# A GRU's difference step that builds its state before its difference, and squares that are issued behind the other set's gates

## The reference, cut to what matters

```
def cell(h, x):
    gi = x @ W_ih + b_ih
    gh = h @ W_hh + b_hh
    r = sigmoid(i_r + h_r)
    z = sigmoid(i_z + h_z)
    n = tanh(i_n + r * h_n)
    h_new = (1.0 - z) * n + z * h
```

## Time and profile before

| what | value |
|---|---|
| median of 3 runs | 2480.27 us (2479.81 to 2484.01) |
| the profiled execution's own time | 2479.73 us |
| its span, first to last instruction | 2478.2 us |
| mean granted TensorE clock | 0.977 |
| busy over the span: PE, DVE, ACT, POOL | 94%, 53%, 27%, 8% |
| L867, `old_less` | 42 instructions, 17.9 us |
| L876, `diff` | 42 instructions, 17.9 us |
| L881, transpose to `hi` | 42 instructions, 18.7 us |
| L731, squares with their accumulator reads | 42 each, 17.4 and 7.5 us |

### The profile page before, as it was taken

How to read it: one execution, slowest core, us unless ns; L and a number is a source line. 1 busy time by engine, 2 the same in 40 slices (tenths; PEclk the granted TensorE clock), 3 DMA queues, 4 the chain that set the end, 5 groups by cost and what they waited for, 6 DMA issues and landing times. The chain is left out here.

```text
span 2478.2 us, 83692 instructions
## 1 busy us (share of the span) xinstructions
PE 2335.3 (94%) x35300; PEld 1277.8 (52%) x35300; DVE 1303.3 (53%) x2691; ACT 661.4 (27%) x1333; POOL 210.6 (8%) x440
## 2 busy tenths in 40 slices
PE   7999999999999989999999999999999999967736
PEld 3444444444444445455666656666666666633312
DVE  4322121212122357777666655666666666888877
ACT  3200000000001123333333333333333333355530
POOL 0000000000000000000000000111111111122225
PEclk9999999999999999999999999999999999999965
DMA  7693131313132445444444443444444444477730
GB/s 236 208 332 127 52 127 52 127 52 127 51 144 103 153 150 152 141 138 134 137 135 135 135 134 101 120 119 116 114 119 119 115 116 118 122 215 232 229 93 5
DMA packets 177335, 330.61 MB, mean 133 GB/s; under 512 B 24272, under 2 KB 87168, under 8 KB 176192
## 3 DMA queue, kind: packets, MB, share of 16 engines
q1 hardware_dynamic: 145360, 267.53, 34.4%
q10 hardware_dynamic: 24192, 44.05, 4.8%
q0 software_dynamic: 7680, 17.57, 4.4%
HBM read 222.39 MB, written 156.77 MB: 153 GB/s over the span
## 5 line engine op out<-in xcount | busy, mean ns | idle before, releaser
L581 PE MATMUL banks<-w_hi,hi 128*32 128x512 f16 (+1 forms) x13824 | 605.0, 328 | 55.7 <-DVE hi L881 43.0
L581 PEld LDWEIGHTS banks<-w_hi,hi 128*32 128x32 f16 x13824 | 359.8, 97 | 284.8 <-DVE hi L881 53.7
L314 DVE SCALAR_TENSOR_TENSOR out_stage<-acc,bias_row 128x512 f32<-128x512 f32 x168 | 116.1, 691 | 622.0 <-PE acc L372 622.0
L581 PE MATMUL banks<-w_hi,lo 128*32 128x512 f16 (+1 forms) x8192 | 354.9, 326 | 0.0
L581 PE MATMUL banks<-w_lo,hi 128*32 128x512 f16 (+1 forms) x8192 | 354.9, 326 | 0.0
L370 PE MATMUL acc<-w_hi,x_even 128*128 128x512 f16 x768 | 291.7, 380 | 13.5 <-DVE x_even L306 11.1
L371 PE MATMUL acc<-w_hi,x_even 128*128 128x512 f16 x768 | 291.6, 380 | 0.0
L372 PE MATMUL acc<-w_lo,x_even 128*128 128x512 f16 x768 | 291.6, 380 | 0.0
L581 PEld LDWEIGHTS banks<-w_lo,hi 128*32 128x32 f16 x8192 | 217.8, 97 | 115.0
L581 PEld LDWEIGHTS banks<-w_hi,lo 128*32 128x32 f16 x8192 | 217.8, 97 | 115.0
L707 ACT ACTIVATE rz<-sums 128x512 f32<-128x512 f32 x176 | 110.9, 630 | 534.5 <-DVE sums L846 534.3
(11 more groups left out here) (172 smaller groups left out, 2162.8 us busy)
## 6 DMA issues: line engine op xcount, KB each, us to landing
stage<-gi_scratch SPq DMA_DIRECT2D x704, 96.0 KB
gi_scratch<-out_stage ACTq DMA_DIRECT2D x168, 256.0 KB, 2.0
stage<-sums_scratch SPq DMA_DIRECT2D x40, 512.0 KB
stage<-in_xT SPq DMA_DIRECT2D x32, 512.0 KB, 6.6
y<-in_x_rows SPq DMA_DIRECT2D x32, 512.0 KB, 4.3
hs_scratch<-h SPq DMA_DIRECT2D x128, 128.0 KB
x_keep<-hs_scratch SPq DMA_DIRECT2D x32, 512.0 KB, 3.9
y<-hs_scratch POOLq DMA_DIRECT2D x32, 512.0 KB
```

The costliest lines, as they stand in the source:

```text
L314: nc.vector.scalar_tensor_tensor(out=out_stage[:, tb], in0=acc[e % BANKS][:], scalar=UNSCALE, in1=bias_row[:].rearrange("p q f -> p (q f)" ...
L581: last = nc.tensor.matmul(bank[q * COLS:(q + 1) * COLS, 0:b - a], state[:, s, j], w[:, j, q * QW + a:q * QW + b], start=first and j == 0, ...
```

## The change

In a DIFFS or LAST step DVE no longer makes `old_less`. It makes the state first (`h` = `new_n` + `z_old`) and then the difference from the state, 256 h less the saved state, and transposes it. On ACT the square of a set's difference is no longer issued behind that set's own tanh, but behind the gates of the other set's next step, in front of the tanh there; the last one of the pass stands behind the loop. The square writes its unused elementwise output into `lo` and not into `rz`.

```diff
-            if mode in (DIFFS, LAST):
-                dve.wait_ge(z_old_ready[s], n)
-                dve.wait_ge(warm_state_loaded[s][u], from_diffs(it) * 8 + 16 * (1 + u))
-                nc.vector.scalar_tensor_tensor(out=old_less[:, s], in0=z_old[:, s], scalar=S_SCALE, in1=warm_state[:, s, u],
-                                               op0=ALU.mult, op1=ALU.subtract).then_inc(old_less_ready[s], 1)
             dve.wait_ge(not_z_ready[s], n)
             dve.wait_ge(n_ready[s], n)
             nc.vector.tensor_tensor(new_n[:, s], not_z[:, s], n_act[:, s], ALU.mult).then_inc(new_n_ready[s], 1)
             dve.wait_ge(z_old_ready[s], n)
             dve.wait_ge(new_n_ready[s], n)
-            if mode in (DIFFS, LAST):
-                dve.wait_ge(old_less_ready[s], from_diffs(it) + (u + 2))
-                nc.vector.scalar_tensor_tensor(out=diff[s], in0=new_n[:, s], scalar=S_SCALE, in1=old_less[:, s],
-                                               op0=ALU.mult, op1=ALU.add).then_inc(diff_made[s], 1)
-                dve.wait_ge(diff_made[s], from_diffs(it) + (u + 2))
-                if mode == DIFFS:
-                    dve.wait_ge(diff_seen[s], from_diffs(it) + (u + 1))
-                nc.vector.transpose(flat(hi[:, s]), diff[s]).then_inc(hi_ready[s], 1)
             if mode not in (HEADS, KEPT):
                 dve.wait_ge(h_stored[s][u], it * 16 + (16 - pair_of(0, 0) * 16))
             if mode == KEPT:
                 dve.wait_ge(state_out_ready[s], it * 2 + (u + 1 - WARM_HEADS))
             nc.vector.tensor_tensor(h_new, new_n[:, s], z_old[:, s], ALU.add).then_inc(h_ready[s], 1)
+            dve.wait_ge(h_ready[s], n)
             if mode in (DIFFS, LAST):
+                dve.wait_ge(warm_state_loaded[s][u], from_diffs(it) * 8 + 16 * (1 + u))
+                nc.vector.scalar_tensor_tensor(out=diff[s], in0=h_new, scalar=S_SCALE, in1=warm_state[:, s, u],
+                                               op0=ALU.mult, op1=ALU.subtract).then_inc(diff_made[s], 1)
+                dve.wait_ge(diff_made[s], from_diffs(it) + (u + 2))
+                if mode == DIFFS:
+                    dve.wait_ge(diff_seen[s], from_diffs(it) + (u + 1))
+                nc.vector.transpose(flat(hi[:, s]), diff[s]).then_inc(hi_ready[s], 1)
                 return
```

```diff
         def act_diff(act, it, u, s):
             act.wait_ge(hi_ready[s], steps_to(it, u) + 2)
-            nc.scalar.activation(rz[:, s, 0:QF], flat(hi[:, s]), ACT.Square,
+
+            nc.scalar.activation(flat(lo[:, s]), flat(hi[:, s]), ACT.Square,
...
-                    act_step(act, it, 1, 0, turns, modes[1], after_tanh=lambda: act_squares(act, T))
-                    if first and modes[1] != FULL:
-                        act_diff(act, it, 1, 0)
...
+                    def gates(u, s, then=None):
+
+                        def after():
+                            if modes[u * s] in (DIFFS, LAST):
+                                act_diff(act, it - 1 if (u, s) == (0, 0) else it, u if s else 1 - u, 1 - s)
+                            if then:
+                                then()
+                        return after
...
+                    act_step(act, it, 1, 0, turns, modes[1], gates(1, 0), lambda: act_squares(act, T))
...
                     with act.Fori(DIFF_TILE, TILES) as i:
                         tile(i, (DIFFS, DIFFS), True)
+                    act_diff(act, pair_of(p, TILES - 1), 1, 1)
```

More of the change, by code:

```diff
@@ L473, in recurrence @@
     new_n = n_sum
-    old_less = sums[:, :, 0:QF]
     diff = [sums[:, s, RZ:RZ + QF // 2].bitcast(F16) for s in range(SETS)]
@@ L517, in recurrence @@
         set_sems(n) for n in ("sums_stored", "gi_kept", "state_out_ready", "state_stored", "diff_seen"))
-    old_less_ready, diff_made = set_sems("old_less_ready"), set_sems("diff_made")
+    diff_made = set_sems("diff_made")
     curves_loaded, split_step = sem("curves_loaded"), sem("split_step")
@@ L794, in tile @@
                     it, T = pair_of(p, i), p * TILES + i
[L795 to L800, removed]
-                    act_step(act, it, 1, 0, turns, modes[1], after_tanh=lambda: act_squares(act, T))
-                    if first and modes[1] != FULL:
-                        act_diff(act, it, 1, 0)
[L804 to L807, removed]
+                    def gates(u, s, then=None):
[5 more added lines that the diff above has]
+                        return after
+                    act_step(act, it, 0, 0, turns, modes[0], gates(0, 0), (lambda: act_signs(act, T - 1)) if routed else None)
+                    act_step(act, it, 0, 1, turns, modes[0], gates(0, 1), lambda: act_sum(act, T))
+                    act_step(act, it, 1, 0, turns, modes[1], gates(1, 0), lambda: act_squares(act, T))
+                    act_step(act, it, 1, 1, turns, modes[1], gates(1, 1, (lambda: act_hit(act, T - 1, i - 2)) if routed else None),
+                             lambda: act_normalise(act, T, i - 1))
                 tile(1, (FULL, FULL), False)
@@ L886, in dve_step @@
             nc.vector.tensor_tensor(h_new, new_n[:, s], z_old[:, s], ALU.add).then_inc(h_ready[s], 1)
+            dve.wait_ge(h_ready[s], n)
             if mode in (DIFFS, LAST):
+                dve.wait_ge(warm_state_loaded[s][u], from_diffs(it) * 8 + 16 * (1 + u))
[5 more added lines that the diff above has]
+                nc.vector.transpose(flat(hi[:, s]), diff[s]).then_inc(hi_ready[s], 1)
                 return
-            dve.wait_ge(h_ready[s], n)
             nc.vector.transpose(flat(h_turned[:, s]), h_new).then_inc(turned[s], 1)
```

## The result

The changed kernel takes 2476.82 us, the kernel before 2480.30 us beside it (20 runs each): ratio 0.9983, 95% interval 0.9977 to 0.9989. It is faster, by 3.5 us and not by the 14.2 forecast, and outside the range of 2460.5 to 2472.

The account below looks back on a forecast made before the run. DVE, nearly full and waiting for the gates, was taken as the bound, not PE. Ten tiles x 0.96 plus nine x 0.51 gave 14.2 us, from 2479.73 to 2465.5, as a median 2466.0; range 2460.5 to 2472.

Parts of the forecast that it names:

- Both waits for the gates: DVE's rn in steps (1,b) and (0,b) would stop waiting for ACT's gates: 0.91 and 0.92 us a tile.
- 0.12 us a tile: In DVE's steps, removing old_less and lengthening the dependent chain would cancel, leaving 0.12 us a tile.
- rival 1, transfers set the tile: In the DIFFS tiles, transfers no denser than 0.85 would hold the tile at 19.8 us: gain 7.4, 2473; chance 0.13.
- nothing queues behind it: On SP, the next load's wait for `hi_ready` follows h by 0.9 us, and nothing would queue behind it.
- The forecast tile of 19.07: A DIFFS tile would shorten from 20.54 to 19.07 us, by 1.47.
- L905 comes at R+5.86+1.27: With R rn's start in (1,a), L905 waits for POOL's normalisation and comes at R+7.13, not R+7.64: gain 0.51.
- nine times 0.51: Gain in the tile's other half, up to L905, in nine of ten tiles: 4.6 us.
- only one tile in ten is late, and as late as before: In the one late tile POOL already sets L905, which waited 0.69 us for the normalisation; that half gains nothing there.
- Rival 4: Later `hi` closes the loop through PE's product and the gates to rn: 13 us lost, 2493; chance 0.07.

Follow-up runs that it names:

- e8: Kernel before with ACT's half of the change only, POOL's scale and shift ahead of its gathers, and late tiles' copies of x issued early: 2465.69 us, 0.9937.
- e5: Changed kernel with POOL's scale and shift ahead of its gathers and late tiles' copies of x issued early, run twice: 2463.96 us, 0.9932; 2462.52 us, 0.9919.
- e3: Changed kernel with POOL making scale and shift ahead of its two gathers: 2472.27 us, 0.9957 to the kernel before.
- e4: Changed kernel with the copies x to y of tiles 21 to 31 issued in tiles 1 to 11: 2469.09 us, 0.9958.
- e2: Kernel before with ACT's half alone, squares behind the other set's gates, old_less kept on DVE: 2479.73 us, 0.9989.
- e9: Changed kernel, POOL's scale and shift first, early copies of x, and only a quarter of the DMA adding states to the output: 2460.75 us, 0.9917.
- e1: Changed kernel with ACT's order of before, so DVE's half of the change alone: 2484.47 us, 1.0012 to the kernel before.
- e7: Kernel before with POOL's scale and shift ahead of its gathers: 2480.51 us, 1.0003.
- e6: Kernel before with the early copies of x alone: 2481.09 us, 1.0001.
- after_again: The changed kernel run once more for a second profile: 2478.43 us, 0.9984 to the kernel before.

## Why the prediction was wrong

*Right: what goes.* Both waits for the gates went, every pitch on DVE came within 0.1, and the operation removed is worth its exposed part only: 0.12 us a tile forecast, 0.19 in e8 against e5, of 1.7 us of busy time. (The prediction's own terms give 0.08 and 0.04 for set a and minus 0.01 for each step of set b, so 0.10.)

*Wrong: "rival 1, transfers set the tile", put at 0.13.* I set against it that DVE never waits for a transfer in the stretch and that a load has a whole step. The first was true of a kernel whose tile was long enough for its transfers; it says nothing of a shorter one. The second left out what a load's issue waits for. The token load isn't issued before the four stores of h have landed, and that took 8.2 us from the last store's issue in place of 4.9; the prediction's "nothing queues behind it" of SP's waits was the same mistake, since the next store and the next sums stand behind this wait. No run changes SP's order alone, so what another order would save stays open. The row with 0.82 and 235 GB/s was the one to go by, as a rate: there was no slack of a fifth in it. The forecast tile of 19.07 needed 235 x 20.54/19.07 = 253 GB/s, and after and e3 stopped at 236 with their loads late. Kind and place were in the rival; its size (gain 7.4) was still too high, since other losses came with it. e4 puts the copies alone at 8 us of the stretch, with the late tile in it.

*Wrong: the term "L905 comes at R+5.86+1.27", nine times 0.51.* The place was right and the size was not: L902 came at R+7.60, not R+7.13, so this half gained 0.04 a tile. R+5.86 was taken as fixed because POOL's chain starts with the routing. But its instructions got longer when they met other instructions of DVE. Before, they were:

```profile
2252.05 0.19 POOL L1112 TENSOR_SCALAR var_eps<-square_sum 128x1 f32<-128x1 f32 x1
...
2252.42 0.58 POOL L1114 TENSOR_TENSOR rstd<-var_eps,neg_half 128x1 f32 x1 [0.18 <-POOL var_eps L1112]
```

and the shift 0.19; after, 0.24, 0.86 and 0.42 in the tile shown above: 0.56 us more. The shift starts 0.05 behind the start of `diff` (2213.83, 0.42) and ends 0.05 behind its end, as if it had been held for it. In the late tile, where DVE stands still, rstd and shift take 0.58 and 0.19 again. The Trainium skill (SBUF — State Buffer, "Summary: rules for kernel authors") has a rule for it: a DVE instruction with two SBUF inputs and a GpSimd instruction that reads SBUF exclude each other, the later one waiting until the first is done. The rows agree. The nearest to a test is e3 against e5: POOL's order is the same, but the shift starts within 0.02 us of the start of `z_old` in e3 and lasts 0.45, and 0.26 behind the start of n_sum in e5 and lasts 0.21. In both it ends some 0.05 behind the end of that DVE instruction. No run was made to isolate it.

*Wrong: that only one tile in ten is late, and as late as before.* It is the same tile as in the earlier trace rows, but POOL's gather is issued 5.4 us late and not 1.2. It is there in both profiles of the changed kernel (5.37, 5.17) and in e2 (6.23), and not in e4 (0.40) or e9 (0.30), which move less. But traffic isn't all: e1 and e7 move as much in a tile as the kernel before and have 0.40 and 0.30 where it has 1.20, and with less traffic e5 still has 3.13 and 2.82, hidden. What POOL waits for there the profile doesn't name, and it stays open.

*Rival 4* had the right price and the wrong loop: in e1 the later `hi` makes rn's wait 0.31 longer in each set-step of b, through square and gates. In the whole change ACT's half removes just this path, so the two halves belong together: ACT's alone is worth 0.5 us of the stretch, DVE's alone minus 4.3, both 4.4.

## What to carry to other kernels

When a wait is removed from a periodic stretch, work out the transfer rate that the shorter period needs before adding up the gain, and take the highest rate that the trace shows over a whole period of that mix as a likely ceiling, whatever the busy share says. Then read what each issue in a DMA queue waits for: here a load whose own 3.9 us hardly changed came late, because its issue waits for stores to land, and what SP issues behind it came late too. List all that joins the loop (here the chain of POOL and the token load) with its distance to the instruction that it feeds, and count its durations as those of one overlap, not as constants. Move copies that can go earlier into a stretch bound by another engine: they were worth nothing before the change and 8 us behind it.

## What the runs showed of the hardware

- The same instruction of POOL on one element a partition took 0.57 to 0.59, 0.67 to 0.69 or 0.85 to 0.86 us (rstd) and 0.19 to 0.47 us (shift), by where DVE's instructions lay; within a profile other than e1's it is the same to 0.02 in nine or ten of ten tiles.
- The granted clock in the window from 2200 to 2340 us is 1.00 before and in e7, and 0.91 to 0.96 in all the others, e6 among them, whose pace is that of the kernel before; PE's busy time is longer in them (100.2 us before, 105.8 after), but that is for the most part the slower clock itself: 1903 matmuls at 52.6 ns each before, 1910 at 55.4 ns after. In e1 (below) a product that had waited 2.40 us for `hi` took 4.46 us, and one behind a wait of 1.31 took 2.78. The granted clock was 0.50 in the middle of the first and 1.00 in the second, the lower and the higher level, 1.2 and 2.4 GHz. The wait ahead of a product doesn't settle it: of e1's ten products behind a wait of 2.40, six took 4.17 to 4.46 and four 2.78, and of those behind 2.06 to 2.09 one of nine was slow in the kernel before and seven of nine in e6. What decides it stays open. It cost little here, since the products have some 3 us of slack: DVE's rn waited for PE at most once in a profile, 0.5 to 1.0 us (after_again, e8, the second e5).

```profile
2243.69 4.46 PE L580 MATMUL banks<-w_hi,hi 128*32 128x512 f16 x64 [2.40 <-DVE hi L882]
...
2254.16 2.78 PE L580 MATMUL banks<-w_hi,hi 128*32 128x512 f16 x64 [1.31 <-DVE hi L882]
...
2306.87 2.78 PE L580 MATMUL banks<-w_hi,hi 128*32 128x512 f16 x64 [2.40 <-DVE hi L882]
```
